# Second cross attention of a two-layer Perceiver: VectorE's small steps behind its maxima, and GpSimd's shares ahead of its other work

## The reference

```python
def _L1_xattn_ref(x, context, Wq, Wk, Wv, Wo, bo):      # x is layer-normed, context is 128 x 257 x 128
    q = (x @ Wq.T).reshape(b, t, h, s)
    k_ = (context @ Wk.T).reshape(b, tc, h, s)
    v = (context @ Wv.T).reshape(b, tc, h, s)
    dot = jnp.einsum('bthd,bchd->bhtc', q * e ** (-0.25), k_ * e ** (-0.25))
    attn = jax.nn.softmax(dot, axis=-1)
    return jnp.einsum('bhtc,bchd->bthd', attn, v).reshape(b, t, e) @ Wo.T + bo
x = x + _L1_xattn_ref(_layernorm(x), ctx_1024, ...)
```

## Time and profile before

| | |
|---|---|
| runs before | 1567.26, 1579.7, 1574.12 us |
| median | 1574.12 us |
| the profiled execution | 1572.63 us |
| its span | 1570.8 us |
| first to last exponential of this block | 642.1 to 1144.4 us |
| PE, DVE, ACT, POOL busy over the span | 81%, 63%, 54%, 53% |

### The profile page before, as it was taken

The page is one execution under the profiler, slowest core; times in us unless marked ns, Lnnn a source line. Parts: engine busy times, 40 slices in busy tenths (PEclk is TensorE's granted clock), DMA queues, the critical chain, the costliest instruction groups (busy, mean ns, idle before and its releaser), DMA issues. The chain is left out here.

```text
span 1570.8 us, 48801 instructions
## 1 busy us (share of the span) xinstructions
PE 1264.7 (81%) x15330; PEld 1097.8 (70%) x15331; DVE 996.1 (63%) x3247; ACT 841.9 (54%) x2658; POOL 835.7 (53%) x1700
## 2 busy tenths in 40 slices
PE   3877788989729996799999999999969878449991
PEld 2655777878629886577777777777758767349991
DVE  4655367877346664577777777777759888433334
ACT  1555256565314443577777777777737665224450
POOL 2555024666636564466666666666534566646661
PEclk9999578788559998899999999999979999569996
DMA  7998552121112121312111111111000000122215
GB/s 223 261 263 218 213 165 76 58 63 53 35 49 73 59 62 37 113 62 91 33 50 33 50 34 43 40 37 43 15 15 3 16 24 23 45 61 68 70 58 169
DMA packets 91997, 122.01 MB, mean 78 GB/s; under 512 B 12689, under 2 KB 67218, under 8 KB 91858
## 3 DMA queue, kind: packets, MB, share of 16 engines
q1 hardware_dynamic: 74194, 82.77, 17.8%
q0 software_dynamic: 12288, 34.82, 7.4%
q10 hardware_dynamic: 5376, 2.63, 0.6%
HBM read 89.68 MB, written 30.49 MB: 76 GB/s over the span
## 5 line engine op out<-in xcount | busy, mean ns | idle before, releaser
L1592 ACT ACTIVATE p_prob<-six,p_nm 128x257 f32<-128x257 f32 x512 | 236.4, 475 | 132.1 <-DVE p_nm L1634 122.2
L1634 DVE TENSOR_REDUCE p_nm<-six 128x2 f32<-128x514 f32 x256 | 164.8, 686 | 12.9 <-PE six L1495 12.8
L1842 PE MATMUL bank<-sb_w,m_experts_aT 128*128 x1152 | 156.6, 279 | 7.6 <-ACT m_experts_aT L1871 4.9
L1821 POOL DMA_INDIRECT expert_outputs<-m_experts_y,m_experts_dest x144 | 142.7, 991 | 25.9 <-POOL m_experts_tiny L1820 11.4
L1858 PE MATMUL six<-m_experts_xT,m_experts_w 128*128 128x128 f32 x1152 | 156.0, 279 | 0.0
L1516 PEld LDWEIGHTS six<-sb_const,p_prob 128*128 128x128 f32 x1024 | 109.5, 141 | 65.5 <-issue 59.1
L1516 PE MATMUL six<-sb_const,p_prob 128*128 128x128 f32 x1024 | 137.0, 277 | 19.3 <-issue 17.5
L1842 PEld LDWEIGHTS bank<-sb_w,m_experts_aT 128*128 128x128 f32 x1152 | 141.1, 193 | 13.0 <-issue 12.8
L776 POOL DMA_INDIRECT expert_inputs<-p_r_x,p_r_slot x128 | 126.0, 984 | 41.2 <-issue 34.5
L1375 POOL TENSOR_TENSOR p_score<-p_score,p_mx 128x512 f32<-128x512 f32 x64 | 67.2, 1049 | 147.8 <-DVE p_mx L1320 145.9
L1858 PEld LDWEIGHTS six<-m_experts_xT,m_experts_w 128*128 128x128 f32 x1152 | 143.3, 196 | 0.6 <-issue 0.2
(11 more groups left out here) (287 smaller groups left out, 3498.2 us busy)
## 6 DMA issues: line engine op xcount, KB each, us to landing
ctxN_ring<-ctxN POOLq DMA_DIRECT2D x32, 516.0 KB, 10.6
ctxT_ring<-ctxT SPq DMA_DIRECT2D x32, 514.0 KB, 12.4
p_ctxT<-ctxT SPq DMA_DIRECT2D x32, 514.0 KB, 3.6
m_experts_x<-expert_inputs SPq DMA_DIRECT2D x144, 64.5 KB
bd_scores<-p_rows SPq DMA_DIRECT2D x32, 256.0 KB, 2.8
p_bd<-bd_scores SPq DMA_DIRECT2D x32, 256.0 KB
sb_w<-w SPq DMA_DIRECT2D x32, 256.0 KB
p_y<-expert_outputs SPq DMA_DIRECT2D x32, 128.0 KB, 3.3
```

Of the source, the lines that this page charges most:

```text
L1592: last = nc.scalar.activation(prob[:, b, g, :], scores_ps[:, g, 0:CTX], ACT.Exp, bias=nm[:, b % 2, g:g + 1], accum_out=total[:, b % 2, g:g ...
L1634: nc.vector.tensor_reduce(nm[:, b % 2, g:g + 2], scores_ps[:, g:g + 2, 0:CTX], AX.X, ALU.max, negate=True).then_inc(s[most], 1)
L1821: nc.gpsimd.indirect_dma_start(m.ys_dram[:, :], bass.IndirectOffsetOnAxis(ap=dest[:, t.par:t.par + 1], axis=0), y[:, t.par, :], None).then ...
L1842: last = nc.tensor.matmul(ps[6 + t.two][:, 0:D], aT[:, t.two, f * P:(f + 1) * P], m.w2[:, DS(held[p] + f * D, D)], start=(f == 0), stop=(f ...
```

## The change

It changes no operation, only the order on two engines.

VectorE: z (slot 0) goes to the front of its slot. zT (slot 1), end values and queries (slot 2) and the residual sum (slot 3) go behind the two maxima of their slot and behind the reciprocal, and stand now ahead of the copy of the turned probabilities. GpSimd: the two spread products go ahead of the weighting of the expert outputs (slot 0) and of X plus bias (slot 1). The waits go with their instructions; those of TensorE and ScalarE stay as they are.

```diff
@@ vector, steps @@
                 for b in range(B4):
+                    if b == 0 and nxt.live:
+                        dve.wait_ge(joined.pool_step, nxt.nth(joined.steps))
+                        if nxt.past(2):
+                            dve.wait_ge(s["zT_ps"], nxt.before(2))
+                        normed(m, z[:, nxt.par, :], nxt, m.RZ).then_inc(s["z"], 1)
                     t, u = near(at, b, -3)
                     if t.live:
                         take_share(t, u)
                         finish(t, u)
+                    if cur.live:
+                        largest(cur, b)
+                    t, u = near(at, b, -1)
+                    if t.live:
+                        dve.wait_ge(s["exp_b"], seq(t, u))
+                        if past(t, u, 2):
+                            dve.wait_ge(s["spread_share"], seq(t, u, 2))
+                        nc.vector.reciprocal(recip[:, u % 2, :], total[:, u % 2, :]).then_inc(s["recip"], 1)
+                    if b == 1 and nxt.live:
+                        dve.wait_ge(s["zT_ps"], nxt.nth())
...
+                        nc.vector.tensor_scalar(zT[:, nxt.par, :], misc_ps, s0, None, ALU.mult).then_inc(s["zT"], 1)
                     if b == 2 and prev.live:
...
                     if b == 2 and nxt.live:
...
                     if b == 3 and prev.live:
...
-                    if cur.live:
-                        largest(cur, b)
-                    t, u = near(at, b, -1)
                     if t.live:
-                        dve.wait_ge(s["exp_b"], seq(t, u))
...
-                        nc.vector.reciprocal(recip[:, u % 2, :], total[:, u % 2, :]).then_inc(s["recip"], 1)
                         dve.wait_ge(s["pT_ps"], seq(t, u))
@@ gpsimd, steps @@
                     done, u = near(at, b, -1)
+                    if done.live:
+                        pool.wait_ge(s["recip"], seq(done, u))
...
+                                                mine, ALU.mult).then_inc(s["spread_share"], 1)
+                        pool.wait_ge(s["spread_share"], seq(done, u))
...
                     t = at(1)
                     if b == 0 and t.live:
                         pool.wait_ge(y_in[t.par], t.nth_of_pair(16))
...
                         nc.gpsimd.tensor_tensor(xb[:, prev.par, :], m.X[:, prev.cols()], m.bX[:, :], ALU.add).then_inc(s["xb"], 1)
-                    if done.live:
-                        pool.wait_ge(s["recip"], seq(done, u))
...
```

## The result

The changed kernel takes 1578.92 us (median of 20 runs, 1571.2 to 1586.05), the kernel before 1573.78 us (20 runs). The ratio is 1.0036, 95% interval 1.0019 to 1.0052, which is 3 to 8 us slower. That is inside the 1% that the prediction called no change, but it has the other sign than the forecast.

A forecast was written before the change was run, and what follows sets the result against it. It took the exponentials' ring and TensorE's own list to set slot lengths. Terms +0.10 and -0.155 gave -0.055 us a tile, by 32 tiles -1.8 us, so 1572 us; range 1563 to 1583.

The forecast's parts named there:

- Slot 2: Queries behind the maxima make TensorE wait before shares: slot 2 gets 0.10 us longer, not 0.70 shorter.
- Slot 3: Residual sum behind the maxima ends, with restart, at 2.42 us, before shares at 2.46: nothing.
- Slots 0 and 1: z ahead of `take_share` fills VectorE's 0.48 us idle, so slot 0's maxima start sooner: mean -0.155 us a tile.
- The step on statistics: Statistics behind the turned copy in slots 1 to 3 feed GpSimd's normalization for z two slots on, with room.
- GpSimd and zT: GpSimd's reordering: nothing, 0.7 us in hand; zT in slot 1 ends before shares, fitting by 0.13 us.
- The signs of being wrong: Shares of slots 1 or 3 wait for VectorE, slot 2 under 4.2 or over 4.7 us, block changes over 8.
- The maxima pay in full: Rival in slot 2: shares would not wait for the queries; with z -19 us, 1555; chance 0.06.
- Restarts are dear: Rival on TensorE's restarts: costs 1% from 0.41 us on; at 0.5, +24 us, 1598; chance 0.08.
- z buys nothing: Rival: something other than z holds slot 0's maxima, leaving only slot 2's term, 1577 to 1581; chance 0.14.

The follow-up runs named there:

- the queries alone: Kernel before with only end values and queries of slot 2 moved behind maxima and reciprocal: 1.0057 times the kernel before, two tiles 32.16 us.
- z back: Changed kernel with z back in its old place, behind `finish` and ahead of the maxima: 1.0046 times the kernel before, two tiles 32.12 us.

## Why the prediction was wrong

**Slot 2** was right in mechanism. TensorE's wait takes the place of ScalarE's, and slot 2 gets longer, not 0.7 shorter. The term was forecast at +0.10 and measured +0.16. Parts of the 0.06: the queries ended at 2.94 instead of 2.93, the restart took 0.10 instead of 0.08, and shares to weighing took 0.90 instead of 0.87, the first transpose behind this wait taking 0.30 instead of 0.27. TensorE's new idle is 0.38, for about 0.5 forecast.

**Slot 3** was forecast at nothing. It is 0.10 shorter ahead of the branch (3.77 to 3.67) and 0.02 longer otherwise. Shares indeed did not wait for the residual sum. What the forecast had not is that slot 2's later weighing reaches into slot 3, as the run with the queries alone shows.

**Slots 0 and 1** are the step that failed: "z now runs before `take_share`, where VectorE stands idle for 0.48". The row of that idle lies behind the loop's branch, and the idle was no slack that z could use: z and the gap that the branch makes come one after the other. I took the label, a wait for TensorE's weighing, at its word; it was true, but it hid the gap. The mean of -0.155 for a tile came out as -0.12 in the mid tile and +0.28 behind the branch, +0.08 in the mean. The step on statistics failed with it: "which the rows show with room" looked at GpSimd, but the statistics are also the last thing ahead of the branch, and 0.2 us later from slot 3's scores (3.31 instead of 3.10), in a slot that was 0.10 shorter, they pushed everything behind it. The maxima of slot 0 in the mid tile start at 0.86, not at the 0.77 that the forecast wanted. And the gain in the mid tile was not z's: it stands with z in its old place.

**GpSimd and zT** at nothing were right; shares of slot 1 start without a wait, and the queries' wait is the one that TensorE shows.

**Sum.** Forecast +0.10 - 0.155 = -0.055 a tile; measured +0.16 - 0.04 + 0.08 = +0.20 by the slots, 0.195 by the cycle, and by 32 tiles 6.2 us, of which the block shows 5.2. The signs of being wrong that the prediction named did not show: slot 2 lies between 4.2 and 4.7, shares of slots 1 and 3 do not wait for VectorE, and the block changed by less than 8. They did not watch slot 0 behind the branch.

**The rivals.** "The maxima pay in full" is refuted by the run with the queries alone. No run left out the wait for the queries, so none shows what two engines in the bank at once would do. "Restarts are dear" would need 0.41 and they cost 0.10. "z buys nothing" was true, but with the branch in the sum its time, 1577 to 1581, holds by luck: it had no term for slot 0 behind the branch.

The trace tells part of what in the branch takes the time. It keeps the instructions of VectorE's own sequencer as well (DVEq), here those of the loop's line for the branch of this slot 0:

```profile
L157 DVEq COMPARE_BRANCH  x1: 56/56/56, 905.0 to 905.0; - x1
L157 DVEq FUSED_REGOPS  x1: 85/85/85, 905.3 to 905.3; - x1
```

The branch itself takes 0.06 us, then the sequencer shows nothing for about a quarter of a microsecond, and then it computes registers. That stretch is there at each of the 12 branches that are taken and missing at the one that is not. What happens in it stays open. The scores behind TensorE's own branch last 0.92 in the changed kernel and 0.93 before, against 0.72 elsewhere and 0.72 where TensorE's branch is not taken, which may be the same cost there; writing out TensorE's steps was not tried.

## What to carry to other kernels

Before an instruction is moved into an idle of its engine, see whether the loop's branch lies in that idle. The label names only the releaser that came last, and comparing with the half of the loop body where no branch lies would not have helped here, for the idle of the mid tile before has the same length and label:

```profile
924.70 0.29 DVE L1619 COPY p_share<-bank 128x128 f32<-128x128 f32 x1 [0.48 <-PE bank L1545]
```

There it was only the wait. When a step stands between two needs, one that waits for what it holds back and one that waits for what it makes, look for a split: half of the reduction was enough for one side to go on, and putting the queries between the halves served both. And when the whole kernel strays by 1%, measure the cycle of the changed stage in the trace; it told 0.1 us a tile apart where medians of 9 to 12 runs could not.

## What the runs showed of the hardware

- A taken loop branch on VectorE: the next instruction started 0.63 us after the start of the last one, be this the statistics (0.45 after its end) or the longer z (0.28 after its end), and 0.83 where the next one was z, against 0.27 for z behind the branch that is not taken and 0.09 in the written-out code. The instructions behind it also followed one another more slowly, 0.41 instead of 0.32 (905.95 to 906.36, against 861.18 to 861.50).
- Writing VectorE's steps out saved 0.28 us for two tiles in the order where a wait of nearly the gap's length lay over it, and 0.57 in the order where the statistics ahead of it came 0.31 later relative to the scores.
- On two chips on which the kernel before takes 1532 and 1574 us, 3% apart, the changed order has the same cycle to 0.01 us (32.12, with z back and as changed).
